# Merged attention stage: scores of odd groups in the other attention's bank, row sums as products with ones

## The reference, cut to what matters

```
scores = jnp.einsum('bkgsd,bktd->bkgst', qg, k) * scale
scores = jnp.where(causal[None, None, None], -jnp.inf, scores)
p = jax.nn.softmax(scores, axis=-1)
out = jnp.einsum('bkgst,bktd->bkgsd', p, v)
```

## Time and profile before

| what | value |
|---|---|
| time, median of 3 runs | 2938.16 us (2936.98 to 2942.46) |
| profiled execution, span from its first to its last instruction | 2941.4 us |
| busy: PE, DVE, ACT, POOL | 91%, 65%, 54%, 45% of the span |
| mean granted clock of PE | 0.965 of full speed |
| the merged attention stage | about 1545 to 2138 us of the span |

### The profile page before, as it was taken

The page is one execution under the profiler, slowest core; times in us unless marked ns, Lnnn a source line. Parts: engine busy times, 40 slices in busy tenths (PEclk is TensorE's granted clock), DMA queues, the critical chain, the costliest instruction groups (busy, mean ns, idle before and its releaser), DMA issues. The chain is left out here.

```text
span 2941.4 us, 48678 instructions
## 1 busy us (share of the span) xinstructions
PE 2672.6 (91%) x16615; PEld 1537.3 (52%) x16876; DVE 1919.5 (65%) x3585; ACT 1595.3 (54%) x3661; POOL 1319.8 (45%) x1344
## 2 busy tenths in 40 slices
PE   6789885799999999869976999998889999999998
PEld 4667672355555555434434666665654444444443
DVE  5778896788787777677656788886473233332335
ACT  7999983565656655464427777776442222222121
POOL 3889896876667766224324111111032222222121
PEclk8999998899999999989987999999989999999999
DMA  4111114322221212150011000000031111121201
GB/s 164 41 52 48 45 37 128 78 44 40 43 39 36 44 38 40 22 172 37 1 36 58 16 20 18 15 16 23 8 97 69 52 49 66 63 69 33 68 33 68
DMA packets 153698, 148.79 MB, mean 51 GB/s; under 512 B 108689, under 2 KB 113169, under 8 KB 151858
## 3 DMA queue, kind: packets, MB, share of 16 engines
q1 hardware_dynamic: 153522, 146.49, 17.6%
HBM read 112.57 MB, written 4.52 MB: 40 GB/s over the span
## 5 line engine op out<-in xcount | busy, mean ns | idle before, releaser
L2101 POOL TENSOR_TENSOR s_state<-s_state,s_ct 128x512 f32<-128x512 f32 x256 | 327.3, 1307 | 80.9 <-DVE s_state L2276 78.6
L806 POOL TENSOR_TENSOR m_aTl<-m_prod,m_aTh 128x512 bf16<-128x512 f32 x88 | 101.8, 1157 | 559.7 <-ACT m_aTh L880 559.7
L2276 DVE TENSOR_TENSOR_SCAN s_state<-s_decay,s_psd 128x512 f32<-128x512 f32 x256 | 301.7, 1208 | 67.8 <-PE s_psd L2421 34.1
L1065 DVE TENSOR_TENSOR m_prod<-m_bank,m_gated 128x512 f32<-128x512 f32 x88 | 60.8, 691 | 406.7 <-ACT m_gated L878 406.7
L878 ACT ACTIVATE m_gated<-m_bank 128x512 f32<-128x512 f32 x88 | 52.5, 597 | 403.1 <-PE m_bank L1196 220.6
L1180 PE MATMUL m_bank<-m_xTl,m_wh 128*128 128x512 bf16 x704 | 267.3, 380 | 3.4 <-ACT m_wh L843 1.0
L1179 PE MATMUL m_bank<-m_xTh,m_wh 128*128 128x512 bf16 x666 | 252.9, 380 | 1.2 <-DVE m_prod L1065 1.2
L2421 PE MATMUL s_psd<-ident,s_v 128*128 128x128 f32 x1024 | 164.5, 285 | 42.4 <-DVE s_state L2276 21.3
L2177 ACT ACTIVATE s_decay<-s_dt,s_nega 128x508 f32<-128x508 f32 x256 | 181.6, 710 | 19.6 <-DVE s_state L2276 19.5
L2190 ACT ACTIVATE s_v<-s_uT,s_bT 128x512 f32<-128x512 f32 x256 | 182.1, 713 | 0.8 <-PE s_psd L2421 0.7
L2421 PEld LDWEIGHTS s_psd<-ident,s_v 128*128 128x128 f32 x1024 | 121.7, 146 | 89.7 <-ACT s_v L2190 46.5
(11 more groups left out here) (515 smaller groups left out, 8021.7 us busy)
## 6 DMA issues: line engine op xcount, KB each, us to landing
s_ct<-ssm_bc SPq DMA_DIRECT2D x64, 256.0 KB, 3.1
m_scale<-moe_scale SPq DMA_DIRECT2D x64, 256.0 KB, 3.1
m_stage<-in_moe_w_dram SPq DMA_DIRECT2D x16, 768.0 KB, 4.7
m_stage<-in_moe_w_dram SPq DMA_DIRECT2D x8, 1024.0 KB, 8.7
X<-in_x_dram SPq DMA_DIRECT2D x4, 1024.0 KB, 11.2
a_cf<-in_ctxT_dram SPq DMA_DIRECT2D x16, 256.0 KB, 2.9
a_wstage<-in_xa_wq_dram SPq DMA_DIRECT2D x8, 512.0 KB, 3.7
a_wstage<-in_xa_wo_dram SPq DMA_DIRECT2D x8, 512.0 KB, 4.3
```

Source lines behind the costliest of these rows:

```text
L2101: pool.tensor_tensor(h, h, ct[t % 4][:, s * P:(s + 1) * P].unsqueeze(1).broadcast_to([P, KB, P]), ALU.mult).then_inc(weighted, 1)
L2276: dve.tensor_tensor_scan(state[i % RING][:, :], decay[t % 2][:, s, :, :].rearrange("p m t -> p (m t)"), ps_d[i % 2][:, :], 0.0, ALU.mult, ...
```

## The change

Three edits. In alone turns the scores of odd groups go to the other attention's `ps_s` (`scores_of`), and `scores` of group g+1 waits for the exponentials of g-1 in place of g. For the first four sequences of the self-attention (`summed`) the exponentials carry no row sum; `values` computes the sums as products of `pT` with a column of ones into the idle `ps_v` of the memory attention, and the reciprocal reads them there. The total of the output weights moves from `mcore.ps_s` to column 16 of `mcore.ps_v`. Two waits are added where the memory attention takes its banks over: its first scores wait for the last alone exponentials of the self-attention, its first values for the last division that reads sums from its bank.

```diff
@@ PairCore.scores
-        if g or late(s, 1):
+        if self.alone(s):
+            if g >= 2:
+                pe.wait_ge(self.exps.sem, self.exps.at(s, g - 1))
+            elif s >= 1:
+                pe.wait_ge(self.exps.sem, self.exps.at(s - 1, 3 + g if self.alone(s - 1) else 4))
+            if g == 1 and s == SEQS - len(self.single):
+                pe.wait_ge(self.other.exps.sem, self.other.exps.at(SEQS - 1))
+        elif g or late(s, 1):
             pe.wait_ge(self.exps.sem, self.exps.at(s, g) if g else self.exps.at(s - 1))
-        bias(self.ps_s[:, :], p)
+        else:
+            pe.wait_ge(self.other.exps.sem, self.other.exps.at(len(self.other.single) - 1))
+        out = self.scores_of(s, g)
+        bias(out[:, :], p)
         k = g if self.KG == 4 else 0
-        mm = three(pe, self.ps_s[:, :].rearrange("p (h t) -> p h t", h=4), (self.qTh[p][:, g, :], self.qTl[p][:, g, :]),
+        mm = three(pe, out[:, :].rearrange("p (h t) -> p h t", h=4), (self.qTh[p][:, g, :], self.qTl[p][:, g, :]),
                    (self.kd[p][:, 0, :, k, :], self.kd[p][:, 1, :, k, :]), False, True)
...
+    def sum_apart(self, s):
+
+        return isinstance(s, int) and s in self.summed
+
+    def scores_of(self, s, g):
+
+        return self.other.ps_s if self.alone(s) and g % 2 else self.ps_s
@@ PairCore.values
             if late(s, 1):
                 pe.wait_ge(self.o_ready.sem, self.o_ready.at(s - 1))
+            elif not self.alone(s):
+                pe.wait_ge(self.other.recip.sem, self.other.recip.at(len(self.other.summed) - 1))
         for h in range(4):
+            if self.sum_apart(s):
+                pe.matmul(self.other.ps_v[:, 4 * g + h:4 * g + h + 1], self.pT[:, h * P:(h + 1) * P], self.ones[:, 0:1],
+                          start=True, stop=True)
@@ PairCore.exponentials
-            e = act.activation(self.prob_of(s, g)[:, h, :], self.ps_s[:, h * P:(h + 1) * P], ACT.Exp,
-                               bias=self.shift[g % 2][:, h:h + 1], scale=self.SCALE,
-                               accum_out=self.total[p][:, 4 * g + h:4 * g + h + 1])
+            column = None if self.sum_apart(s) else self.total[p][:, 4 * g + h:4 * g + h + 1]
+            e = act.activation(self.prob_of(s, g)[:, h, :], self.scores_of(s, g)[:, h * P:(h + 1) * P], ACT.Exp,
+                               bias=self.shift[g % 2][:, h:h + 1], scale=self.SCALE, accum_out=column)
@@ PairCore.maxima
-        dve.tensor_reduce(self.top[:, :], self.ps_s[:, :].rearrange("p (h t) -> p h t", h=4), AX.X,
+        dve.tensor_reduce(self.top[:, :], self.scores_of(s, g)[:, :].rearrange("p (h t) -> p h t", h=4), AX.X,
@@ PairCore.divide
-        dve.reciprocal(self.rtotal[:, :], self.total[p][:, :]).then_inc(self.recip.sem, 1)
+        total = self.other.ps_v[:, 0:16] if self.sum_apart(s) else self.total[p][:, :]
+        dve.reciprocal(self.rtotal[:, :], total).then_inc(self.recip.sem, 1)
@@ stage_pair
-        core = PairCore(fr, st, "b", 1, PairCore.HW ** -0.5, ps_t, 1, range(0, LAG))
+        core = PairCore(fr, st, "b", 1, PairCore.HW ** -0.5, ps_t, 1, range(0, LAG), range(0, LAG))
-        mcore = PairCore(fr, st, "c", 4, 1.0, ps_t, 64, range(SEQS - LAG, SEQS))
+        mcore = PairCore(fr, st, "c", 4, 1.0, ps_t, 64, range(SEQS - LAG, SEQS), ())
         core.second, mcore.second = mcore.prob, core.prob
+        core.other, mcore.other = mcore, core
+        core.ones = ones
-            dve.tensor_scalar(sw[:, 3:4], mcore.ps_s[:, 0:1], 1.0 / (sizes[3] * P), 1e-5, ALU.mult, ALU.add).then_inc(wscale, 1)
+            dve.tensor_scalar(sw[:, 3:4], mcore.ps_v[:, 16:17], 1.0 / (sizes[3] * P), 1e-5, ALU.mult, ALU.add).then_inc(wscale, 1)
-            pe.matmul(mcore.ps_s[:, 0:1], ones[:, :], wsum[:, 3:4], start=True, stop=True).then_inc(wo_total, 1)
+            pe.matmul(mcore.ps_v[:, 16:17], ones[:, :], wsum[:, 3:4], start=True, stop=True).then_inc(wo_total, 1)
```

More of the change, by code:

```diff
@@ L2549, with __init__ @@
     GH, HW = 4, 32
-    def __init__(self, fr, st, tag, key_groups, scale, ps_t, key_count, single):
-        self.single, self.second = single, None
+    def __init__(self, fr, st, tag, key_groups, scale, ps_t, key_count, single, summed):
+        self.single, self.second, self.other = single, None, None
+        self.summed, self.ones = summed, None
         self.fr, self.KG, self.SCALE, self.ps_t = fr, key_groups, scale, ps_t
```

## The result

The changed kernel takes 2948.34 us (median of 20 runs) against 2940.28 for the kernel before (20 runs): ratio 1.0018, 95% interval 1.0011 to 1.0025, so about 5 us slower by the ratio (the medians lie 8 us apart, because the changed kernel's times form two groups). The forecast was 2934.7 us, range 2928 to 2942.

A forecast was written before the change was run, and what follows sets the result against it. Bounds: a chain of waits in turns 0 to 2, PE nearly in turn 3 and in memory alone turns. 4.6 us gained less 2.46 for sums gives 2.1, plus 1.4: 3.5 off 2938.2, so 2934.7 us, range 2928 to 2942.

The forecast's parts named there:

- PE in turns 0 and 1 at full clock, which is a choice: Self-attention's turns 0 and 1: assumed full PE clock when timing the groups; needed each turn done in 19.3 us.
- the free scalings at (1,1) and (2,1): DVE's small scaling falls while POOL awaits its next chunk; exponentials start at 1571.45 (was 1576.94) and 1593.7 (was 1600.47).
- third rival: At (0,3) POOL goes on first, so the scaling waits 3.0 us more: 0.8 gained, 2937.4 us; chance 0.17.
- the walk: Start times of exponentials computed group by group through turns 0 to 3: 4.6 us gained on entering turn 3.
- second rival: PE's clock too low in turns 0 and 1: at 0.60, 2945 us; decides below about 0.61; chance 0.13.
- The big gains given back at the next group: Gains of 5.5 us at (1,1) and 6.8 at (2,1) shrink to 1.2 and 3.4 next group, through continuous POOL work.
- Reads gone: Exponentials of sequences 0 to 3 lose accumulator reads: 0.1 us each, 0.4 a group, 1.0 in place of 1.4.
- The sums' price: Sixty-four one-column products, each with its own weight load: 0.82 us a group taken, bounded by nothing and 1.75.
- fourth rival: Products sharing an operand share its weight load, so sums cost nothing: 2.46 us back, 2932.2 us; chance 0.05.
- Paid in turn 3: PE bounds turn 3, so the sums of (3,0) and (3,1) cost 1.64 us there.
- Memory turns: Memory attention's alone turns 16 to 19, given the second bank: 0.2 us gained at 16, 1.2 at 19, sum 1.4.
- The first rival, the seam: DVE's held scaling slips between two POOL instructions; (1,2) and (2,2) start about 3 us earlier each: 2928.7 us; chance 0.20.

The follow-up runs named there:

- extra products: Changed kernel with ten more products ahead of PE's waits for keys of sequences 1, 2 and 3: ratio 0.9999; eight in the kernel before: 0.9988.
- three ties won: Changed kernel with three added POOL waits, its chunks starting after the scalings of (0,3), (1,1) and (2,1): ratio 1.0004.
- one tie alone: Changed kernel with one added POOL wait, its second chunk starting only after the scaling of (0,3): ratio 1.0016.
- low run: A later profiled execution of the unaltered changed kernel, from the faster of its two groups of times: 2938.53 us.

## Why the prediction was wrong

The step that failed is "PE in turns 0 and 1 at full clock, which is a choice", with what hung on it: the free scalings at (1,1) and (2,1), and the third rival's price, "everything to turn 3 is 2.7 later". Measured, turns 0 and 1 ran at 0.72 and 0.71, and the scalings of (1,1) and (2,1) were held 2.35 us each, while those of (1,2) and (2,2) were free: the reverse of the walk. Between the two executions of the changed kernel the difference at (4,0) is 12.6 us, not 2.7.

The second rival had the right sign and, by luck, nearly the time, 2945; its condition, a clock below 0.61, was not met. I had asked only whether PE's sum of work fits a turn. But PE needn't fill the turn: sums and values stand between one group's transposes and the next scores, and at 1.2 GHz their 3.27 us in place of 1.70 make the scaling miss POOL. The late keys then keep PE waiting, it goes on at 1.2 GHz, and the next tie is lost. I priced the clock and the lost tie as two rivals with chances of their own; they are one chain. By the runs, extra products (1.0018 to 0.9999), the scaling on ACT (to 0.9995) and three ties won (to 1.0004) each give back some 4 to 7 us of the same loss, the ties with 4 either way, and the products help the kernel before as well; one tie alone gives nothing that the ratio shows. Products and scaling on ACT together (0.9974) bring it to where the banks alone are. How the loss divides between clock and ties is open.

Point by point:

- **The banks: a gain, and larger.** Alone they gave 0.9979, 6 us with 2.8 either way. Entry of turn 3, (3,1): 66.67 us after the first exponentials in place of 70.37, 3.7 gained; 4.6 was forecast with the reads. One profile each doesn't settle this: the run of the last section, with the instructions of before, has 67.10.
- **The big gains given back at the next group:** with the banks alone 3.9 gained at (1,1) and 1.0 at (1,2), so the size was right, but the reason was PE's clock and not POOL. At (2,1) and (2,2) it was 4.7 and 3.7, where 6.8 and 3.4 were forecast.
- **Reads gone:** the four exponentials take 1.14 us to the end of the last, so they start 0.26 apart, as expected; but the sums alone show no gain from it, and with the extra products the sums of four sequences cost 1.6 in a thousand against none (0.9999 and 0.9983, with 0.0013 either way), about 5 us.
- **The sums' price:** right at full clock. 0.445 us for a sum and its values at full clock (1.78 a group, 0.96 more than the values' 0.82); 1.5 a group at 1.2 GHz, inside the bounds. Each loads its weights itself, against what the Trainium skill (TensorE: Matmul & The Clock Gate, section "Part 2: What happens when you issue a matmul") let one hope, so the fourth rival is out.
- **Paid in turn 3:** 0.9 at full clock, not 1.64. In the changed kernel, at 0.90, the turn took 27.46 us, 3.3 more than before (24.20); in the low run, at 0.86, it took 29.13. The 1.00 of the earlier trace rows was lost too.
- **`keys`:** the wait of the earlier trace rows is gone (1627.86, right behind the values), as forecast, though late.
- **Memory turns:** 1.1 gained in the changed kernel, 1.4 in the low run, 1.4 forecast.
- **The first rival, the seam:** out; the scaling was held through two POOL instructions.

What stays open: why PE's clock rises some 2 us earlier, counted from the first exponentials, in one execution than in another, although the exponentials and transposes start alike. No run here shows it.

## What to carry to other kernels

Work put on an idle engine is not free when it stands between one step's result and the next step's start: price it at the lower clock that the rows show for that stretch, and follow whom it makes late. Where two engines meet within 0.2 us, a forecast has two outcomes, and rivals that push the same tie are priced together. Run the halves of a double edit apart: here one was worth 6 us, and the other turned it into a loss.

## What was not expected of the hardware

One profiled execution is less than it seems. The run with two banks for the memory turns only has the kernel before's instructions in turns 0 to 3, yet its scaling of (1,1) was not held:

```profile
1571.43 0.17 DVE L2700 TENSOR_SCALAR b_shift<-b_top 128x4 f32<-128x4 f32 x1
1571.64 0.37 ACT L2676 ACTIVATE c_prob<-b_pss,b_shift 128x128 f32<-128x128 f32 x1
1571.64 2.14 POOL L112 TENSOR_TENSOR c_wvl<-ahead,c_wvh 128x1024 bf16<-128x1024 f32 x1 [3.62 <-ACT c_wvh L102]
```

It came 0.21 us ahead of POOL, where the earlier trace rows shows it 0.64 behind, and (3,0) came 60.49 us after the start and not 64.03. So some 3.5 of the 5.5 us that the walk meant to gain at (1,1) can be there without the change. The profile that the walk was built on was itself one of the slower executions: by the runs that give both, a span lies 1.8 us under its time (2936.7 and 2938.53 in the low run), so its 2941.4 stands for some 2943, where the 20 times of the kernel before run from 2935.1 to 2944.5.
